# Two-layer graph network on one core: the order and the sharing of the first four row tiles' sums at the start of the first product

## The reference, cut to what matters

```
h = jnp.maximum(_layernorm(x, axis=-1), 0.0)          # x is 2048 x 512
x = x + _L0_gnn_ref(h, adj, adj)                      # adj is 2048 x 2048
...
# _L0_gnn_ref(x, Coefficient2, A):
def adjacent_mat(adj):
    adj = adj + jnp.eye(adj.shape[0], dtype=adj.dtype)
    deg = jnp.sum(adj, axis=1)
    dinv = jnp.where(deg > 0, deg ** (-0.5), 0.0).astype(adj.dtype)
    return dinv[:, None] * adj * dinv[None, :]
adj = adjacent_mat((A_c + A_c.T) * 0.5)
y = Coefficient2 @ adj
y = y @ x
```

## Time and profile before

| | |
|---|---|
| median of 3 runs | 864.47 us (863.64 to 864.56) |
| the profiled execution's own time | 864.24 us |
| its span in the trace | 862.4 us |
| PE busy | 840.7 us (97%) |
| DVE busy | 703.1 us (82%) |
| ACT busy | 428.9 us (50%) |
| granted TensorE clock, whole span | 1.00 |

### The profile page before, as it was taken

How to read it: one execution, slowest core, us unless ns; L and a number is a source line. 1 busy time by engine, 2 the same in 40 slices (tenths; PEclk the granted TensorE clock), 3 DMA queues, 4 the chain that set the end, 5 groups by cost and what they waited for, 6 DMA issues and landing times.

```text
span 862.4 us, 15281 instructions
## 1 busy us (share of the span) xinstructions
PE 840.7 (97%) x5207; PEld 756.5 (88%) x5207; DVE 703.1 (82%) x1220; ACT 428.9 (50%) x797; POOL 281.4 (33%) x299
## 2 busy tenths in 40 slices
PE   2999999999999999999999999999999999999998
PEld 2888888888888888887899999999999999999786
DVE  6899886557656885587999999998999999998864
ACT  3445333321111111257776666666666666785753
POOL 0000000000000000066875555555566644556332
PEclk9999999999999999999999999999999999999999
DMA  9979831703222222053300000000000032000144
GB/s 348 406 278 377 346 98 62 206 0 122 97 98 98 97 97 74 1 195 125 129 27 23 16 26 26 25 24 24 26 26 25 22 87 75 25 2 2 49 147 148
DMA packets 37674, 87.95 MB, mean 102 GB/s; under 512 B 7216, under 2 KB 8368, under 8 KB 37616
## 3 DMA queue, kind: packets, MB, share of 16 engines
q1 hardware_dynamic: 37616, 87.24, 29.0%
HBM read 74.45 MB, written 12.78 MB: 101 GB/s over the span
## 4 chain that ended last, share of the span: by engine, by line
PE 95%; DVE 2%; DMA 1%; ACT 1%; issue 0%; ACTq 0%
PE bank L1861 28%; PE bank L1905 14%; PE bank L77 13%; PE bank L79 13%; PE bank L78 13%; PE bank L554 3%; PE bank L1066 1%; PE bank L1067 1%; PE bank L1071 1%; PE bank L2439 1%; PE bank L2378 1%; PE bank L2435 1%; PE bank L2433 1%; DMA l_h<-x 1%; PE bank L1018 1%; DMA l_src<-e_rows 0%
## 5 line engine op out<-in xcount | busy, mean ns | idle before, releaser
L1381 DVE SCALAR_TENSOR_TENSOR l_q<-bank,e,mask 128x512 fp32r<-128x512 f32 x512 | 339.1, 742 | 23.0 <-PE bank L1861 23.0
L1861 PE MATMUL bank<-l_parts,l_q 128*128 128x260 f32 x2048 | 249.8, 283 | 0.0
L1861 PEld LDWEIGHTS bank<-l_parts,l_q 128*128 128x128 f32 x2048 | 246.7, 188 | 0.6 <-issue 0.2
L77 PE MATMUL bank<-x_hi,s_hi 128*128 128x512 f32 x448 | 174.5, 389 | 0.0
L79 PE MATMUL bank<-x_hi,s_lo 128*128 128x512 f32 x448 | 174.3, 389 | 0.0
L78 PE MATMUL bank<-x_lo,s_hi 128*128 128x512 f32 x448 | 174.3, 389 | 0.0
L800 POOL TENSOR_TENSOR l_prod<-wh,l_a 128x512 f32<-128x512 f32 x29 | 34.1, 1194 | 381.5 <-ACT wh L757 381.5
L1549 ACT ACTIVATE l_o_q<-bank 128x260 f32<-128x260 f32 x128 | 49.1, 389 | 103.7 <-PE bank L1861 96.5
L79 PEld LDWEIGHTS bank<-x_hi,s_lo 128*128 128x128 f32 x448 | 84.1, 188 | 17.5
L78 PEld LDWEIGHTS bank<-x_lo,s_hi 128*128 128x128 f32 x448 | 84.1, 188 | 17.5
L77 PEld LDWEIGHTS bank<-x_hi,s_hi 128*128 128x128 f32 x448 | 84.1, 188 | 17.2
(11 more groups left out here) (229 smaller groups left out, 1183.1 us busy)
## 6 DMA issues: line engine op xcount, KB each, us to landing
rows<-adj_t SPq DMA_DIRECT2D x48, 512.0 KB, 3.7
l_now<-adj SPq DMA_DIRECT2D x16, 512.0 KB, 7.0
l_rows_k<-adj_t SPq DMA_DIRECT2D x16, 512.0 KB, 7.8
l_src<-e_rows SPq DMA_DIRECT2D x32, 256.0 KB, 3.1
l_kept<-adj SPq DMA_DIRECT2D x12, 512.0 KB, 12.9
wh_store<-wh SPq DMA_DIRECT2D x4, 1040.0 KB, 6.2
l_h<-x SPq DMA_DIRECT2D x4, 1024.0 KB, 17.0
x<-x SPq DMA_DIRECT2D x1, 4096.0 KB, 13.5
```

The costliest lines, as they stand in the source:

```text
L77: pe.matmul(acc, hi, rhs_hi, start=first, stop=False, skip_group_check=True)
L1381: v.scalar_tensor_tensor(out=q[:, i, :], in0=bank[S_BANKS[hh]][:], scalar=e[:, i, H + h:H + h + 1], in1=mask[:, i, cols], op0=ALU.is_le, o ...
L1861: return pe.matmul(bank[Q_BANKS[hh][t]][:, 0:PW], q[:, i, t * P:(t + 1) * P], parts[pair_slot][:, i, hh * PW:(hh + 1) * PW], start=i == 0, ...
```

## The change

- `CHUNKS` gets five entries: x comes in tiles (0, 2), (2, 4), (4, 8), (8, 12), (12, 16). The second chunk's load stands behind `now` of tile 1 in SyncE's queue.
- Tile 0: the kept half is loaded and summed in two pieces of 512 columns, and `degree(0)` runs between them; `guard` adds the last piece's sum.
- Tiles 1 to 3: ScalarE sums the rows of `rows_k` and of the kept half by two copies with `accum_out` (`sum_kept`; the copies themselves go into parts of `G` that nobody reads), and `degree` and `guard` take these sums. VectorE's `add_kept(i)` comes a tile later, behind `invert_root(i + 1)`; that of tile 3 stands behind `cut_lo(4)`.
- ScalarE's queue: for tiles 2 and 3 `sum_kept`, `cut_hi`, one `normalise`, `take_root`, `cut_x_hi`. `cut_hi(5)` comes after five of the eight bank copies.
- `refine` has a step less. `invert` makes `fall` = −degc/4, `correct` multiplies y by `pos`, and `scale` ends the correction: the same number of instructions after the root, one more (`fall`) before it.
- `load(i)` of tiles 4 and on waits for `add_kept(i - 4)` as well.

```
-    CHUNKS = ((0, 4), (4, 8), (8, 12), (12, 16))
+    CHUNKS = ((0, 2), (2, 4), (4, 8), (8, 12), (12, 16))
...
+    now_loaded = (first_loaded, x_loaded[1], x_loaded[2], x_loaded[4])
+    def now_count(i):
+        return (1, 3, 4, 6)[i] if i < EARLY else 2 * i + 1
+    def kept_count(i):
+        return (2, 5, 7, 8)[i] if i < EARLY else 2 * i + 2
+    def root_count(i):
+        return 3 * i + 1 if i < EARLY else i + 2 * EARLY - 1
...
                 sp.wait_ge(deg_ready, DEG * before + 1)
+                sp.wait_ge(summed, kept_count(before))
                 sp.wait_ge(lo_ready, (before if before < EARLY else before + EARLY) + 1)
...
+            if i == 1:
+                load_x(1)
+            sp.dma_start(rows_k[:, b, :], adj_t[tile, second]).then_inc(sums_loaded[b] if i else x_loaded[3], 16)
+            if i == 0:
+                sp.dma_start(kept_half(0)[:, 0:F], adj[tile, GW:GW + F]).then_inc(x_loaded[3], 16)
+                sp.dma_start(kept_half(0)[:, F:GW], adj[tile, GW + F:N]).then_inc(sums_loaded[0], 16)
+            else:
+                sp.dma_start(kept_half(i), adj[tile, second]).then_inc(sums_loaded[b], 16)
...
             if n == 1:
-                v.tensor_tensor(to, yy, yy, ALU.mult).then_inc(ln_chain, 1)
+                v.scalar_tensor_tensor(out=to, in0=yy, scalar=-0.5, in1=yy, op0=ALU.mult, op1=ALU.mult).then_inc(ln_chain, 1)
...
+        def add_first_kept():
+            v.wait_ge(x_loaded[3], 32)
+            add_kept_columns(0, slice(0, F), part_more[:, 0, 0:1]).then_inc(ln_chain, 1)
+            link("first_kept")
+            degree(0)
+            v.wait_ge(sums_loaded[0], 16)
+            add_kept_columns(0, slice(F, GW), part_more[:, 0, 1:2]).then_inc(summed, 1)
         def add_kept(i):
+            if i < EARLY:
+                v.wait_ge(sums_loaded[i], 32)
+                v.wait_ge(scalar_chain, root_count(i) - 1)
+            add_kept_columns(i, slice(0, GW), part[:, i, 1:2]).then_inc(summed, 1)
...
         def invert(i):
-            v.wait_ge(root_ready, i + 1)
+            v.wait_ge(deg_ready, DEG * i + 2)
+            v.tensor_scalar(fall[:, i, :], degc[:, i, :], -0.25, None, ALU.mult).then_inc(deg_ready, 1)
+            v.wait_ge(scalar_chain, root_count(i))
             v.reciprocal(y[:, i, :], droot[:, i, :]).then_inc(inv_chain, 1)
...
+        add_now(0)
+        add_first_kept()
+        guard(0)
+        invert_root(0)
+        cut_lo(0)
+        cut_x_lo(0)
+        add_now(1)
+        statistics(1)
+        variances(1)
+        degree(1)
+        guard(1)
+        invert_root(1)
+        refine(1, 0)
+        cut_lo(1)
+        refine(1, 1)
+        cut_x_lo(1)
+        refine(1, 2)
+        for i in range(2, EARLY):
+            add_now(i)
+            if i == 2:
+                refine(1, 3)
+                refine(1, 4)
+            degree(i)
+            guard(i)
+            invert_root(i)
+            add_kept(i - 1)
             cut_lo(i)
             cut_x_lo(i)
+        cut_lo(4)
+        add_kept(3)
         add_now(4)
-        cut_lo(4)
         add_kept(4)
         degree(4)
         guard(4)
-        statistics(1)
         cut_lo(5)
-        variances(1)
+        statistics(2)
+        variances(2)
...
+        def sum_kept(i):
+            a.wait_ge(sums_loaded[i], 32)
+            for n, source in enumerate((rows_k[:, i, :], kept_half(i))):
+                at = GW // F * (2 * i - 2 + n)
+                spare = G[:, at:at + GW // F, :].rearrange("p b f -> p (b f)")
+                a.activation(spare, source, ACT.Copy, accum_out=part_more[:, i, n:n + 1]).then_inc(scalar_chain, 1)
...
+        cut_hi(1)
+        sum_kept(1)
+        take_ln_root(1)
+        take_root(1)
+        cut_x_hi(1)
+        for i in range(2, EARLY):
+            sum_kept(i)
             cut_hi(i)
+            normalise(1, i, i + 1)
             take_root(i)
             cut_x_hi(i)
         cut_hi(4)
-        keep_first_part()
+        keep_first_part(range(5))
         cut_hi(5)
+        keep_first_part(range(5, G8))
```

More of the change, by code:

```diff
@@ L136, in smooth_features @@
     droot = sb("l0_droot", [P, T, 1])
+    fall = sb("l0_fall", [P, T, 1])
+    part_more = sb("l0_part_more", [P, EARLY, 2])
     y = sb("l0_y", [P, T, 1])
@@ L279, in add_now, with add_kept_columns @@
                                    accum_out=part[:, i, 0:1]).then_inc(summed, 1)
-        def add_kept(i):
-            if i == 0:
[L282 to L288, removed]
+        def add_kept_columns(i, cols, total):
+            return v.scalar_tensor_tensor(out=kept_half(i)[:, cols], in0=rows_k[:, i % SLOTS, cols], scalar=1.0,
+                                          in1=kept_half(i)[:, cols], op0=ALU.mult, op1=ALU.add, accum_out=total)
@@ L291, in guard @@
             v.wait_ge(deg_ready, DEG * i + 1)
-            v.tensor_scalar(degc[:, i, :], deg[:, i, :], TINY, None, ALU.max).then_inc(deg_ready, 1)
-            v.tensor_scalar(pos[:, i, :], deg[:, i, :], 0.0, None, ALU.is_gt).then_inc(deg_ready, 1)
+            if i == 0:
+                v.wait_ge(summed, kept_count(0))
+            elif i < EARLY:
+                v.wait_ge(scalar_chain, root_count(i) - 1)
+            v.tensor_scalar(degc[:, i, :], deg[:, i, :], rest, TINY, ALU.add, ALU.max).then_inc(deg_ready, 1)
@@ L298, in square, with invert_root @@
             v.wait_ge(inv_chain, INV * i + 1)
-            v.scalar_tensor_tensor(out=ytmp[:, i, :], in0=y[:, i, :], scalar=degc[:, i, :],
+            v.wait_ge(deg_ready, DEG * i + 4)
+            v.scalar_tensor_tensor(out=ytmp[:, i, :], in0=y[:, i, :], scalar=fall[:, i, :],
                                    in1=y[:, i, :], op0=ALU.mult, op1=ALU.mult).then_inc(inv_chain, 1)
         def correct(i):
-            v.wait_ge(inv_chain, INV * i + 2)
-            v.tensor_scalar(ytmp[:, i, :], ytmp[:, i, :], -0.25, 1.5, ALU.mult,
-                            ALU.add).then_inc(inv_chain, 1)
+            v.wait_ge(deg_ready, DEG * i + 3)
+            v.tensor_tensor(y[:, i, :], y[:, i, :], pos[:, i, :], ALU.mult).then_inc(inv_chain, 1)
         def scale(i):
             v.wait_ge(inv_chain, INV * i + 3)
[L307 to L318, removed]
+            v.scalar_tensor_tensor(out=dinv[:, i, :], in0=ytmp[:, i, :], scalar=1.5,
+                                   in1=y[:, i, :], op0=ALU.add, op1=ALU.mult).then_inc(inv_chain, 1)
+        def invert_root(i):
             invert(i)
@@ L322, in vector @@
             scale(i)
+        statistics(0)
+        variances(0)
+        for n in range(5):
+            refine(0, n)
+        add_now(0)
[24 more added lines that the diff above has]
+            add_kept(i - 1)
             cut_lo(i)
             cut_x_lo(i)
+        cut_lo(4)
+        add_kept(3)
         add_now(4)
-        cut_lo(4)
         add_kept(4)
@@ L366, in vector @@
         cut_x_lo(8)
-        statistics(2)
+        statistics(3)
         invert(7)
-        variances(2)
+        variances(3)
         square(7)
@@ L374, in vector @@
         scale(7)
-        refine(2, 0)
-        statistics(3)
-        refine(2, 1)
+        refine(3, 0)
+        statistics(4)
+        refine(3, 1)
         cut_lo(10)
-        refine(2, 2)
+        refine(3, 2)
         cut_x_lo(10)
-        refine(2, 3)
-        variances(3)
-        refine(2, 4)
+        refine(3, 3)
+        variances(4)
+        refine(3, 4)
         add_now(8)
-        refine(3, 0)
-        refine(2, 5)
-        refine(3, 1)
+        refine(4, 0)
+        refine(4, 1)
         add_kept(8)
-        refine(3, 2)
+        refine(4, 2)
         degree(8)
-        refine(3, 3)
+        refine(4, 3)
         guard(8)
-        refine(3, 4)
+        refine(4, 4)
         cut_lo(11)
-        refine(3, 5)
         cut_x_lo(11)
@@ L459, in take_root @@
             a.wait_ge(deg_ready, DEG * i + 2)
-            a.activation(droot[:, i, :], degc[:, i, :], ACT.Sqrt, scale=0.5).then_inc(root_ready, 1)
+            a.activation(droot[:, i, :], degc[:, i, :], ACT.Sqrt, scale=0.5).then_inc(scalar_chain, 1)
+        def sum_kept(i):
[4 more added lines that the diff above has]
+                a.activation(spare, source, ACT.Copy, accum_out=part_more[:, i, n:n + 1]).then_inc(scalar_chain, 1)
         def cut_hi(s):
             a.wait_ge(slot_free, s + 1)
+            if s < EARLY:
+                a.wait_ge(summed, now_count(s))
+            elif s < FIRST_NOW:
+                a.wait_ge(summed, kept_count(s - EARLY))
+            elif s < FIRST_LATE:
+                a.wait_ge(summed, now_count(s - EARLY))
             a.activation(s_hi[:, s % 2, :], step_source(s), ACT.Copy).then_inc(hi_ready, 1)
@@ L468, in cut_x_hi, with keep_first_part @@
             a.activation(hi, h[:, i, :], ACT.Relu, scale=dinv[:, i, :]).then_inc(x_hi_ready, 1)
-        def keep_first_part():
-            for k in range(G8):
+        def keep_first_part(banks):
+            for k in banks:
                 wait_for_sum(a, EARLY - 1, k)
@@ L502, in scalar @@
         cut_x_hi(9)
```

(10 more changed lines are left out.)

73 lines of the change are left out of this document (37 added, 36 removed).

## The result

The changed kernel takes 865.58 us (median of 20 runs, 864.81 to 866.33) against 864.39 (20 runs, 863.53 to 865.39) for the kernel before: the ratio is 1.0014, 95% interval 1.0008 to 1.002. That is 1.19 us slower, within the range 863.4 to 867.0 and within the 0.2% that I called no change, but above the 864.9 that I had forecast. The interval lies clear of 1, so it is a small loss and not nothing.

A forecast was written before the change was run, and what follows sets the result against it. PE's matmul stream was taken to bound the kernel; a start 2.2 us earlier is spent on waits until step 3 starts 0.47 us late, so 864.24 + 0.47 = 864.7, as a median 864.9 us, range 863.4 to 867.0.

The forecast's parts named there:

- the first matmul: Sign in the trace after: PE's first matmul starts at 13.0 to 13.8 us.
- the wait before step 2: Sign in the trace after: PE waits about 1.1 us for `early_hi` before step 2.
- What bounds it: Whole kernel: PE, busy 97% of the span, sets the time through its first matmul's start plus a fixed amount of work.
- The first tile, 2.2 us earlier: Tile 0: smaller first load of x and shorter norm let step 0 start at about 13.3, 2.2 us earlier.
- Tile 1, a wait of 0.2: Tile 1: PE can start step 1 at 21.3, after step 0 ends at 21.1, a wait of 0.2 us.
- Tile 2 at 27.95: Tile 2: load at 22.1, then ScalarE's sums, cut, norm and root; step 2 starts at 27.95 after waiting 1.1 us.
- Tile 3 at 34.73: Tile 3: behind VectorE's deferred add, step 3 starts at 34.73 after waiting 1.3 us more, 0.47 us later than before.
- Behind step 3: After step 3: nothing gives the half microsecond back and nothing is added; step 6 has 0.2 us of slack.
- Rival A: Steps 0 to 3: the lead survives, step 3 starts at 32.0, 2.2 us earlier, for 862.2 us; chance 5%.
- B: ScalarE's sums: accumulating copies are dear, 1.6 us each gives 865.8, 1.9 each gives 866.4; chance 15%.
- C: PE's clock: falls again once after the stops of 1.1 and 1.3 us, for 867.3 us; chance 7%.
- D: Steps 5 to 8: little slack and loads waiting for deferred sums cost 1 to 2 us more, 866.4; chance 10%.

The follow-up runs named there:

- the probe: One-column GpSimd memsets waiting for each load, added to the kernel before and to the changed kernel; no ratio, tile 2's last piece landed 0.64 us later after the change.
- x_in_four: Changed kernel with x loaded and normed in four row tiles again, plus landing probes: 1.0016 of the kernel before.
- the adds in the gap: Changed kernel with VectorE's add_kept of tiles 1 and 2 moved between guard and the next tile's root answer: 864.68 us, 0.9999 of the kernel before.

## Why the prediction was right, and where it was off

The time lies in the range and the mechanism is the one forecast: the early start is spent at tiles 2 and 3, on ScalarE's queue in front of the root and on VectorE's deferred add, and three experiments that each take one thing off this path (one sum, the norm, the deferred add) each bring the time back to that of the kernel before. Two of the signs that I gave missed: the first matmul (14.55, not 13.0 to 13.8) and the wait before step 2 (0.27, not 1.1). Term by term:

- *What bounds it*: right. PE's stream decides: step 4 starts 1.19 us later (40.89 − 39.70), and the time is longer by about as much.
- *The first tile, 2.2 us earlier*: off; 1.00 was measured (15.55 to 14.55). The term was the landing. x itself came earlier than I had it (4.43, not 4.99) and the norm took 2.9 us instead of 2.7, but what then held DVE were the next loads. I had `now` of tile 0 at 7.63 and the kept half's first piece at 9.61; DVE waited for them until 8.86 and 10.75 (timeline of DVE, changed kernel):

```profile
8.86 1.23 DVE L294 SCALAR_TENSOR_TENSOR l_now<-rows,l_now 128x1024 f32<-128x1024 f32 x1 [1.50 <-DMA l_now<-adj]
...
10.75 0.69 DVE L298 SCALAR_TENSOR_TENSOR l_kept<-l_rows_k,l_kept 128x512 f32<-128x512 f32 x1 [0.66 <-DMA l_kept<-adj]
```

  The second of these sets the first matmul: 1.14 late there, 1.25 late at step 0. The kernel before's `now` landed at 9.48 by the probe, where my rate would give 8.95: pieces at the head of the queue don't land evenly. The error cost nothing in the sum, because both of the waits that I had forecast before step 2 lie behind it and took it up (0.27 us in all instead of 1.3); it was not foreseen.
- *Tile 1, a wait of 0.2*: none. Its tile was a microsecond late as well (`early_hi` at 21.41, so PE could start at 22.28 instead of 21.3, for the last piece was there at 17.84 and not 16.9), but step 0 ended later still (22.70).
- *Tile 2 at 27.95*: 28.57. **The term that was mis-sized is the landing of tile 2's last piece: 22.1 in the sum, 23.01 measured.** Of the 0.9 the probes put 0.64 on the change itself, which I had taken as neutral to the loads; x_in_four puts them on x's small chunks. The landing goes through one for one when ACT's queue is what ends last: with it at 22.77 (the adds in the gap) `early_hi` of tile 2 starts at 27.45, with 23.01 at 27.70. The sums were 2.10 instead of 2.3 (1.06 and 1.04 from start to start; the read-out of 0.19 is overlapped), which took 0.2 back; cut, norm and root were as forecast.
- *Tile 3 at 34.73*: 35.33, all of it inherited. From one `scale` to the next I had 6.78 us; it was 6.76.
- *Behind step 3*: right that nothing is given back or added, but for 0.12: the step behind a wait is longer (5.56), which I hadn't counted. With the 0.60 of step 3, that is the whole of 1.19 − 0.47 = 0.72. For step 6 I had 0.15 us of slack (50.9 against 51.05); `s_lo` was there at 51.5 and step 6 began at 51.8.
- *Rival A* (lead kept) fell; *B* (dear sums) fell, as a copy with its sum costs 1.06; *C* fell, since the 24 matmuls behind the longer wait take 5.56 us, 0.23 each, which is the 2.4 GHz level. The Trainium skill (TensorE: Matmul & The Clock Gate, Why this matters for your kernels) warns of idle gaps between bursts of matmuls; behind the gaps of 0.27 and 1.04 us here no row shows the lower level. *D* fell, since PE has no wait behind step 3 in this stage and the loads for tile 5 were issued at 28.89, in time.
- The rule of the Trainium skill (ScalarE: Activation LUTs, Rules for kernel authors: adds on VectorE) agrees with the runs. With the sums back on VectorE the kernel is 1.8 us faster than the changed one on the same chip, more than the 1.15 that I had allowed it. The rows show two things that go beyond the single pass: ACT's norm lies beside VectorE's sum, and the deferred add no longer comes on top. How the rest divides between them is not measured.

What stays open: what the later landing alone costs, with the early start kept, and why the DMA engines move less behind a smaller first load of x. The runs show it (283 against 390 GB/s from 4 to 6 us, and the landing back at 22.27 with x in four tiles), but no run tells the size of the DMA from its place in the queue. The landing differs by up to 0.4 us between executions (22.77 to 23.18 over kernels with the same loads, and 0.3 for tile 1 in the kernel before), which limits such splits.

## What to carry to other kernels

Before work is moved to an idle engine, write down that engine's queue between the wait for the load and the instruction that the bound engine waits for: ACT was busy for half of the span, but at tile 2 everything it was given stood in front of a root of 0.19 us. An earlier start is worth only what the slowest tile-to-tile path (here 6.76 against 5.44 us) lets through, so compare the periods first and the start last. Two reorderings that each used the same idle gap of VectorE didn't add: the first had made it too short for the second.

## What the runs showed that I had not expected

- A copy with a row sum costs ScalarE only 0.1 us more than a plain one: 1.06 and 1.04 us from start to start for 1024 columns, with the read-out of 0.19 overlapped, against 0.95 for `s_hi` (25.11 to 26.06).
- With x's first load halved, tiles 1 to 3 landed 0.65 us later in the probed pair, with the DMA engines as busy. From 4 to 6 us the queue moved 213 to 320 GB/s in every execution with a first load of x of 512 KB or less, and 390 to 411 in the three with 1 MB.
- A PE step that begins with a wait is 0.1 us longer: its first eight matmuls show 2.08 instead of 1.98 us. The weight load in front of it then starts 0.03 us before the matmul (35.30 for 35.33) and not 0.22 (22.48 for 22.70); that this is the cause isn't shown.
- Step 0, about half of it at the 1.2 GHz level, took 7.1 to 8.3 us from execution to execution. Where no wait follows, that moves everything behind it, by as much as the change did.
